# First layer of a two-layer convolution kernel: the next image's scale made at chunk 13, three resident chunks, and its first chunk rounded before the present image is done

## The reference

```python
def _L0_conv_ref(x, weight, bias):
    x_q = _quantize(x, S_X)          # clip(round(x / 0.05), -128, 127)
    w_q = _quantize(weight, S_W)
    acc = lax.conv_general_dilated(x_q, w_q, window_strides=(1, 1), padding=((1, 1), (1, 1)), ...)
    out_fp = acc * (S_X * S_W) + bias[None, :, None, None]
    out_q = jnp.clip(jnp.round(out_fp / S_OUT), QMIN, QMAX)
    return out_q * S_OUT

# _gn(v): (v - mean) / sqrt(var + 1e-5) over each group of 2 channels of one image
x = x + _L0_conv_ref(_gn(x), L0_conv_weight, L0_conv_bias)
x = x + _L1_conv_ref(_gn(x), L1_conv_conv_w, L1_conv_conv_b)
```

## Time and profile before

| | |
|---|---|
| median of 3 runs | 5598.68 us (5594.73 to 5600.21) |
| profiled execution | 5597.51 us, its span 5595.8 us |
| first layer's part of the span | about 2311 us (layer 1's first DMA goes out at 2311.4) |
| PE busy | 5111.7 us, 91% of the span |
| DVE busy | 4613.7 us, 82% |
| ACT busy | 4026.4 us, 72% |
| b_stream loads | 168 of 1024 KB; b_x loads 276 of 1024 KB; b_x stores 128 of 2048 KB |

### The profile page before, as it was taken

How to read it: one execution, slowest core, us unless ns; L and a number is a source line. 1 busy time by engine, 2 the same in 40 slices (tenths; PEclk the granted TensorE clock), 3 DMA queues, 4 the chain that set the end, 5 groups by cost and what they waited for, 6 DMA issues and landing times.

```text
span 5595.8 us, 110144 instructions
## 1 busy us (share of the span) xinstructions
PE 5111.7 (91%) x43848; PEld 3713.1 (66%) x43848; DVE 4613.7 (82%) x5393; ACT 4026.4 (72%) x2541; POOL 1164.8 (21%) x1323
## 2 busy tenths in 40 slices
PE   0989898989898989499999899999899899899899
PEld 0434343434343434289889799889799799799898
DVE  6889898989898976788788788788688788788786
ACT  1767676767676767378788688688688788788786
POOL 0000000000000000233333233233233233333233
PEclk9999999999999999799999999999999999999999
DMA  7979797979797955699999999999999999999997
GB/s 288 364 291 393 288 398 280 405 276 405 280 405 278 403 223 233 159 186 183 190 187 175 198 172 177 201 178 180 186 182 170 200 173 182 192 182 181 196 171 119
DMA packets 796691, 1333.32 MB, mean 238 GB/s; under 512 B 61080, under 2 KB 585880, under 8 KB 718952
## 3 DMA queue, kind: packets, MB, share of 16 engines
q0 software_dynamic: 185888, 539.06, 41.7%
q1 hardware_dynamic: 585232, 599.40, 37.6%
q10 hardware_dynamic: 25024, 187.38, 10.1%
HBM read 786.73 MB, written 538.84 MB: 237 GB/s over the span
## 4 chain that ended last, share of the span: by engine, by line
PE 47%; DMA 6%; SPq 2%; DVE 2%; issue 1%; ACT 1%; ACTq 0%; POOL 0%; DVEq 0%; POOLq 0%
PE c_tps L1214 35%; DMA c_x<-out_dram 6%; PE c_cps L1193 4%; PE c_cps L1194 4%; PE c_cps L1195 4%; SPq L860 2%; DVE c_z L1116 0%; ACT c_z L1075 0%; ACT c_feat L1089 0%; DVE c_feat L1147 0%; ACTq L959 0%; DVE s_gs_half L265 0%; ACT c_xr L1102 0%; DVE c_feat L1150 0%; DVE rstd L1173 0%
## 5 line engine op out<-in xcount | busy, mean ns | idle before, releaser
L1214 PE MATMUL c_tps<-c_feat,c_tt 123*128 123x256 f16 (+1 forms) x20736 | 2395.7, 274 | 103.0 <-ACT c_xr L1102 91.7
L1214 PEld LDWEIGHTS c_tps<-c_feat,c_tt 123*128 123x128 f16 (+1 forms) x20736 | 2003.6, 98 | 368.4 <-issue 102.2
L508 PE MATMUL b_ps<-b_xq,w0main 128*128 128x512 bf16 x9168 | 2002.2, 381 | 150.1 <-ACT b_haloq L442 150.1
L508 PEld LDWEIGHTS b_ps<-b_xq,w0main 128*128 128x128 bf16 x9168 | 891.5, 97 | 1255.8 <-ACT b_haloq L442 131.1
L1031 POOL DMA_DIRECT2D out_dram<-c_xr x1152 | 1057.6, 1054 | 2128.2 <-DVE c_xr L1162 1677.2
L1075 ACT ACTIVATE c_z<-c_x,c_rs 128x976 f16<-128x976 f32 x576 | 1151.0, 1999 | 165.8 <-DMA c_x<-out_dram 165.8
L1116 DVE SCALAR_TENSOR_TENSOR c_z<-c_x,c_rs,c_z 128x976 f16<-128x976 f32 x576 | 1104.4, 1918 | 126.2 <-ACT c_z L1075 106.0
L1162 DVE TENSOR_SCALAR c_xr<-c_tps 57x1024 f32<-57x1024 f32 (+1 forms) x576 | 701.1, 1217 | 479.4 <-PE c_tps L1214 433.5
L450 ACT ACTIVATE b_q<-b_ps,q_bias 128x1024 int8<-128x1024 f32 x512 | 567.3, 1110 | 599.8 <-PE b_ps L508 570.5
L1102 ACT ACTIVATE c_xr<-c_tps 57x1024 f32<-57x1024 f32 (+1 forms) x576 | 638.7, 1109 | 421.5 <-PE c_tps L1214 401.1
L1089 ACT ACTIVATE c_feat<-c_cps 122x1024 f16<-122x1024 f32 x576 | 822.8, 1429 | 155.6 <-PE c_cps L1195 123.6
(11 more groups left out here) (146 smaller groups left out, 1446.9 us busy)
## 6 DMA issues: line engine op xcount, KB each, us to landing
out_dram<-b_x POOLq DMA_DIRECT2D x128, 2048.0 KB, 8.1
out_dram<-c_xr POOLq DMA_DIRECT2D x576, 384.0 KB, 7.6
c_x<-out_dram SPq DMA_DIRECT2D x220, 912.0 KB, 21.0
b_stream<-in_x_dram SPq DMA_DIRECT2D x168, 1024.0 KB, 9.8
b_x<-in_x_dram ACTq DMA_DIRECT2D x138, 1024.0 KB, 9.1
b_x<-in_x_dram SPq DMA_DIRECT2D x138, 1024.0 KB, 8.8
out_dram<-c_xr POOLq DMA_DIRECT2D x512, 72.0 KB, 8.8
c_tt<-table_scratch ACTq DMA_DIRECT2D x56, 576.0 KB
```

The costliest lines, as they stand in the source:

```text
L508: last = pe.matmul(ps[:, g % 3, j, :], k.w0main[:, y, d, :, :].rearrange("p o r -> p (o r)"), row(2 * i + j + y - 1)[:, d:d + W], start=(y ...
L1214: last = pe.matmul(tps[:, s % 2, o % 4, :], tt[0:rows, o, tp, 2 * d:2 * d + 2, :].rearrange("k w m -> k (w m)"), feat[0:rows, (e * N + i) ...
```

## The change

- RESIDENT goes from 4 to 3: chunk 3 of the next image is streamed too (13 streamed chunks instead of 12 for each of 7 images). Every chunk is taken a step sooner: two takes at steps 11 and 12, one at step 13, none at 14 and 15.
- DVE: `means` and `vector_spread` move from step 14 to step 13 (STAGE), `vector_variance` stands right behind `vector_spread`, before the chunk's statistics; `new_scales` moves to step 14, before the additions of chunk 14.
- PE: the two products stand behind groups 0 and 2 of chunk 14 (g = 56 and 58), not behind the image.
- ACT: the root stands at step 16 between `round_out(14, 2)` and `round_out(14, 3)`. At step 17 `round_x(b+1, 0)` stands ahead of `round_out(15, 0)`, and `widen_x(b+1, 0)` and `halo(b+1, 0, 0)` stand between `round_out(15, 1)` and `round_out(15, 2)`. The body of the next image starts at `round_x(1)`.
- PSUM slots: group 63 goes to slot 1 instead of 0, so that group 0 of the next image has slot 0; group 63 then waits for the rounding out of 61, group 0 for that of 60 of the image before, groups 1 and 2 for all of it.

```diff
-RESIDENT = 4
+RESIDENT = 3
...
+        STAGE = N - X_SLOTS + 3 + RESIDENT - 1
+        RING = 3
...
+            return 1 if g == G * N - 1 else g % RING
...
-                act.wait_ge(conv_done, b * (G * N) + max(0, G * (n - XQ_SLOTS + 1) + 1) + START)
+                act.wait_ge(conv_done, b * (G * N) + (max(0, G * (n - XQ_SLOTS + 1) + 1) if n or first else G * (1 - XQ_SLOTS) + 1) + START)
...
+            def next_image(b):
+                widen_x(b + 1, 0)
+                halo(b + 1, 0, 0)
...
+                    early = more and n == N + 1 and STAGE + 3 < N + 1
+                    if early:
+                        round_x(b + 1, 0)
-                    if n < N:
+                    if 1 <= n < N:
                         round_x(b, n)
                     if n >= 2:
                         round_out(b, n - 2, 0)
                         round_out(b, n - 2, 1)
...
+                    if early:
+                        next_image(b)
...
                         round_out(b, n - 2, 2)
+                        if more and n == STAGE + 3:
+                            gs.scalar(act, b + 1)
                         round_out(b, n - 2, 3)
...
-                if more:
-                    gs.scalar(act, b + 1)
...
-                        pe.wait_ge(out_rounded, b * (G * N) + max(0, g - 2) + START)
+                        freed = g - 1 if g == G * N - 1 else 0 if g == 1 else g - 2 if g else -RING
+                        pe.wait_ge(out_rounded, b * (G * N) + freed + RING + START)
...
-                if more:
-                    gs.tensor(pe, b + 1)
+                        if more and n == STAGE + 1 and i in (0, 2):
+                            gs.tensor(pe, b + 1, (i // 2,))
...
-                    if more and n == N - 2:
+                    if more and n == STAGE:
                         last.then_inc(all_taken, 1)
...
                         means(b + 1)
+                    if more and n == STAGE + 1:
+                        new_scales(b + 1)
...
-                    if more and n == N - 2:
+                    if more and n == STAGE:
                         gs.vector_spread(dve, b + 1, mv_x)
-                    if more and n == N - 1:
-                        new_scales(b + 1)
+                        gs.vector_variance(dve, b + 1)
...
-                    if more and n == N - 2:
-                        gs.vector_variance(dve, b + 1)
```

More of the change, by code:

```diff
@@ L266, in vector_rstd, with tensor @@
         self.link(dve, t, 8, dve.reciprocal(self.rstd[:, :], self.half[:, :]))
-    def tensor(self, pe, t):
-        for i, rhs in enumerate((self.own_mean, self.spread)):
+    def tensor(self, pe, t, parts=(0, 1)):
+        for i in parts:
+            rhs = (self.own_mean, self.spread)[i]
             pe.wait_ge(self.given, t * 2 + i + 1 + START)
@@ L374, in load_ahead, with ps_slot @@
                 load_chunk(eng, next_x, b, m - N, h)
+        def ps_slot(g):
+            return 1 if g == G * N - 1 else g % RING
         TAKEN = [[RESIDENT + n] if n < STREAMED else [] for n in range(N)]
@@ L425, in round_x, with widen_x, halo @@
                                scale=scale).then_inc(rounded, 1)
-            def widen_x(b, n):
+            def widen_x(b, n, first=False):
                 act.wait_ge(rounded, b * N + n + 1 + START)
-                act.wait_ge(conv_done, b * (G * N) + max(0, G * (n - XQ_SLOTS + 1) + 1) + START)
+                act.wait_ge(conv_done, b * (G * N) + (max(0, G * (n - XQ_SLOTS + 1) + 1) if n or first else G * (1 - XQ_SLOTS) + 1) + START)
                 act.activation(xq[:, n % XQ_SLOTS, :, 1:W + 1], x8[:, :, :], ACT.Identity).then_inc(cast, 1)
-            def halo(b, h, n):
+            def halo(b, h, n, first=False):
                 act.wait_ge(halo_scales, b + 1 + START)
                 act.wait_ge(halo_loaded, (2 * b + h + 1) * HALO + START)
-                act.wait_ge(conv_done, b * (G * N) + START)
+                act.wait_ge(conv_done, b * (G * N) + (0 if h or first else 1 - G * N) + START)
                 act.wait_ge(cast, b * N + n + 1 + START)
@@ L449, in round_out @@
                     act.wait_ge(added, b * (2 * N) + max(0, g // 2 - 1) + START)
-                act.activation(q8[:, i // 2, 2 * (i % 2):2 * (i % 2) + 2, :], ps[:, g % 3, :, :], ACT.Identity,
+                act.activation(q8[:, i // 2, 2 * (i % 2):2 * (i % 2) + 2, :], ps[:, ps_slot(g), :, :], ACT.Identity,
                                bias=k.q_bias[:, :], scale=S_X * S_W / S_OUT).then_inc(out_rounded, 1)
+            def next_image(b):
+                widen_x(b + 1, 0)
+                halo(b + 1, 0, 0)
             def body(b, more):
@@ L455, in body @@
                     load_ahead(act, b, n + X_SLOTS - 5, more, 1)
-                    if n < N:
+                    early = more and n == N + 1 and STAGE + 3 < N + 1
+                    late = more and n == N + 1 and not early
+                    if early:
+                        round_x(b + 1, 0)
+                    if 1 <= n < N:
                         round_x(b, n)
@@ L460, in body @@
                         round_out(b, n - 2, 1)
-                    if n < N:
+                    if 1 <= n < N:
                         widen_x(b, n)
-                    if n == 0:
-                        halo(b, 0, n)
+                    if early:
+                        next_image(b)
                     if n == 8:
@@ L468, in body @@
                         round_out(b, n - 2, 2)
+                        if more and n == STAGE + 3:
+                            gs.scalar(act, b + 1)
                         round_out(b, n - 2, 3)
+                    if late:
+                        round_x(b + 1, 0)
+                        next_image(b)
                 load_ahead(act, b, N + AHEAD - 1, more, 1)
-                if more:
-                    gs.scalar(act, b + 1)
             load_first(act, 1)
             act.wait_ge(first_read, N - AHEAD + START)
+            act.sem_inc(out_rounded, RING)
             gs.scalar(act, 0)
+            round_x(0, 0)
+            widen_x(0, 0, True)
+            halo(0, 0, 0, True)
             with act.Fori(0, nb - 1) as b:
@@ L507, in body @@
                                 for d in range(3):
-                                    last = pe.matmul(ps[:, g % 3, j, :], k.w0main[:, y, d, :, :].rearrange("p o r -> p (o r)"),
+                                    last = pe.matmul(ps[:, ps_slot(g), j, :], k.w0main[:, y, d, :, :].rearrange("p o r -> p (o r)"),
                                                      row(2 * i + j + y - 1)[:, d:d + W], start=(y == 1 and d == 0), stop=(y == 2 and d == 2))
                         last.then_inc(conv_done, 1)
-                if more:
-                    gs.tensor(pe, b + 1)
+                        if more and n == STAGE + 1 and i in (0, 2):
+                            gs.tensor(pe, b + 1, (i // 2,))
             gs.tensor(pe, 0)
```

2 lines of the change are left out of this document (1 added, 1 removed).

## The result

The changed kernel takes 5566.88 us (median of 5 runs, 5553.23 to 5573.55) against 5597.36 us (5 runs): a ratio of 0.9945, 95% interval 0.9929 to 0.9961. It is faster, by 30 us (0.55%) where I forecast 76, and its time lies 5 us above my range. The profiled execution took 5564.92 us, its span is 5563.3.

A forecast was written before the change was run, and what follows sets the result against it. PE was taken as the bound, with a 21.0 us gap per image boundary. Six looping images save 10.3 each (62), the last 21.7, image 0 loses 7.7: together 76 us, giving 5522 us, range 5487 to 5562.

The forecast's parts named there:

- The gap of 21 us goes, with a cover of 1.1 us: Image boundary: widening and halo end at about 659.1, PE wants them at 660.2, so PE's 21.0 us gap goes.
- PE stands 5.2 us in order for the mean: At the first product behind group 56, PE waits 5.2 us for the mean, with groups 57 to 63 queued behind.
- DVE's stand for the variance: Behind the second product, DVE stands from 636 until about 640.8, up to 4.8 us; its round has room.
- The start of the next image, 5.0 us: At six looping boundaries PE stands 2.1 us for ACT's rounding plus 2.9 for a jump; 2.1 at the seventh.
- that rival (9.0 us): PE's jump back is as long as in layer 1, 8.3 to 9.0 us, giving 5548 us; chance 0.17.
- Slow starts, 1.7 + 0.8: PE's clock falls behind waits: 1.7 us lost behind the mean's wait, 0.8 at the next image's start.
- DVE's round, 258 us, is hidden: Per image DVE needs 258 us, 259 at most, below PE's round; it catches up by step 10 or 12.
- both its cases: Stream turnaround bounds DVE and the kernel gets slower: mild (5545 to 5587 us) chance 0.08, slower 0.05.
- the products (0.8): PE's two products themselves cost 0.3 and 0.4 us, taken as 0.8 with semaphores.
- the last boundary and image: From the end of image 6 to that of 7, no jump and no product: 251.2 us, saves 21.7.
- turnaround, mild: Milder case of the stream's turnaround bounding DVE: 5545 to 5587 us; landings of 13.0 us give 5560; chance 0.08.
- signs of being wrong: PE's jump above 6 us, stream landings exceeding 13 us, or ACT's halo coming after group 63.

The follow-up runs named there:

- the short stream: The changed kernel with each half of the stream buffer loading one row instead of four, a quarter of the stream's bytes: 5550.71 us (0.9911).
- the four pieces: The changed kernel with the stream buffer in four pieces of 512 KB instead of two of 1 MB, same bytes: 5549.16 us (0.9907).
- the later products: The changed kernel with PE's two products behind groups 58 and 59 instead of 56 and 58: 5546.62 us (0.9905).
- the new order on ACT: The changed kernel with ACT's rounding of group 0 ahead of the widening of chunk 1, instead of behind the rounding of chunk 2: 5575.67 us (0.9954).

## Why the prediction was wrong, step by step

- *The gap of 21 us goes, with a cover of 1.1 us*: right; the cover was 1.6, and without the early rounding it is 10.2 us again.
- *PE stands 5.2 us in order for the mean*: right, 5.3 in the first image, up to 7.4 where DVE lagged. DVE's stand for the variance: 4.8 forecast, 5.4 measured, and harmless to the time: taking it away gained nothing.
- *The start of the next image, 5.0 us*: a mis-sized term. The chain was right: 1.9 without jumps against the 1.76 measured where the loops are written out. The jump was not: I took DVE's 2.9 us for ACT, and ACT's is 5.7. At the second boundary PE loses 672.14 - 652.71 - 11.7 = 7.7 us in all. At the first it stands 2.45 + 3.70, because the groups between were slow and filled the rest. PE's own jump, 3.7 at most, lies within this; that rival (9.0 us) was wrong for this layer.
- *Slow starts, 1.7 + 0.8*: a mis-sized term, and the largest part of the miss. There are up to three in an image, not one and a half. At the first boundary of the changed kernel 36 matmuls behind the wait for the mean took 365.65 - 354.91 = 10.7 us where 7.8 are due (2.9 more), three groups behind the jump 401.4 - 387.9 = 13.5 where 11.7 are due (1.8), and groups 3 to 56 212.0 where 210.2 are due (1.8): 6.5 against 2.5. The granted clock in the first two of these stretches is 0.72 and 0.87. Counted like this the six images lose 4.4 to 7.6 us, 5.9 on the mean.
- *DVE's round, 258 us, is hidden*: this is the step whose mechanism failed. I noted nearly the right size for the landing at full DMA rate, 12.4 us (12.1 to 13.0 measured), and gave the turnaround 0.13 for both its cases; what I missed is that it also bars the catching up, even below the point at which it would set the whole image. DVE starts some 10 us later against PE (its first take comes 19.8 to 20.8 us behind PE's first matmul, 10.5 to 10.8 before; I had reckoned 12) and has to make this up by step 12; in image 2 a streamed step took DVE 15.2 to 16.5 us, of which 14.3 are work. So in three of six images, 2 to 4, the double takes found it late: PE stood at group 55 too (878.59 above). These three take 271.1 to 271.2 us each; with the short stream they take 265.0 to 267.4, 15 us less in all, while the other three change by 1.2 us at most.

The account of the first full image: 249.1 of matmuls, 5.7 for the mean at its end (5.2 forecast), 0.3 for the products (0.8), 2.45 + 3.70 at the boundary (5.0), 6.5 slow (2.5), together 267.8 of the 268.3 measured, against 262.6.

The six images together take 1971.06 - 354.47 = 1616.6 us by the first products, against 6 x 262.6 = 1575.6: 41 us too long. By the same counting 21 of these are slow starts, 10 the stands at groups 51 and 55, 6 the start of the image, 4 the wait for the mean, less 3 for the products; 3 are not placed. Some 4 us come back ahead of and behind these six images (the last boundary and image took 251.0 us, forecast 251.2), so the first layer gained 38.6 instead of 76; and 6 us went in the second layer.

Put by experiment, the turnaround costs the changed kernel 16 to 18 us as it stands (the short stream, the four pieces); that fits the 15 us of the images 2 to 4. The larger part, some 25 us, is the slow starts and ACT's jump, which PE's rows show. Writing the loops out took the jumps of all engines away together; no experiment took the slow starts away by themselves, so their share rests on PE's rows. What the stream takes back of other gains is 9 us of the later products and all 22 of the new order on ACT.

The rival "turnaround, mild" (5545 to 5587), at 0.08, names the place where 5567 fell. Its mechanism was at work: it asked for landings of 13.0 us, and the images 2 to 4 have 12.9 to 13.0. But it put the whole loss on this, and removing the waits wins only 16 us back; that its number fits is for the larger part luck. Of my signs of being wrong, landings above 13 us came, up to 15.1 in the streamed steps. My range left most of this rival out.

## What to carry to other kernels

When a gap that stood once per iteration is closed, list what was hidden in it, engine by engine: every engine's jump back, the first pass of each chain, the slow start, and the time in which the slowest follower caught up; each was free before. A buffer that is reloaded only once it is read has a turnaround that caps the speed of catching up, not only the steady speed; smaller pieces lifted that cap here at the same bytes. And a product whose input comes late belongs behind work that doesn't need it: on an in-order engine its place in the queue is a wait for everything behind.

## What the hardware showed that I had not expected

- A jump back in the same layer costs 2.9 us on DVE, 2.45 to 3.7 on PE and 5.7 (6.2 at most) on ACT; PE stood 9.0 in the second layer. The Trainium skill, "Runtime: NRT & Kernel Launch", section "Instruction fetch mechanics", names the stall of a taken branch whose target has to be fetched. These traces give the sizes of the waits, and the waits of all three by "issue" are gone where the loops are written out; that the fetch is what the engines wait for, no row shows.
- The length of a stand does not tell whether a slow start follows. Behind the stand of 2.45 us at 387.86 the next 54 matmuls lost 1.8 us, at a granted clock of 0.87; behind another of 2.45 us, at 1468.05, and behind that of 3.46 us at 656.17, they lost 0.2 at 1.00: the first three matmuls cover 0.82 us there, that is 2.4 GHz, where 1.46 is the lower level.
- The same stretch moves 405 to 410 GB/s with halves of 1 MB and 419 to 424 with pieces of 512 KB, both at a DMA share of 1.00 to 1.02; and the changed kernel, with halves, moved 432 GB/s from 656.17 to 668.02 at a share of 1.02. So a share of 1 did not mean that DMA gave all it could, and neither was the 422 of the first read the earlier trace rows the top.
- With the first layer's loops written out, the untouched second layer took 3272 to 3279 us in four kernels; with the loops kept it took 3283 to 3296 in thirteen. In the profiled executions of the kernel before and of its version without loops, 3.8 of the 6.8 us between them lie there. Why is open.
